# One core: shared weights in the local-attention value products, halves swapped for half of the heads, and one loop in place of two

## The reference, cut to what matters

```python
qkv = x @ Wqkv                      # 16 heads of 64
q, k = rotary(l2norm(q) * qs), rotary(l2norm(k) * ksc)
# windows of w = 32 tokens, so nw = 4 windows in 128 tokens
bk2, bv2 = look(bk), look(bv)       # each window sees itself and the window before it: 64 keys
mask = (it < jb) | (it > jb + w) | (jb == -1)
sim = where(mask, -max, einsum('bhwie,bhwje->bhwij', bq, bk2) * 8)
out = einsum('bhwij,bhwje->bhwie', softmax(sim), bv2)
x = out.reshape(b, n, 1024) @ Wo + x
```

## Time and profile before

| what | value |
|---|---|
| median of three runs | 1504.75 us |
| the profiled execution's own time | 1506.91 us |
| its span, first to last instruction | 1504.0 us |
| PE busy | 1419.3 us, 94% |
| DVE, ACT, POOL busy | 1310.1, 1269.5, 1179.5 us |
| `values`, records of L1246 on PE | 12288, 376.4 us busy (they overlap) |
| mean granted clock of TensorE | 0.985 |
| transfers `vs<-v` | 96 of 384 KB, 3.3 us to landing |

### The profile page before, as it was taken

How to read it: one execution, slowest core, us unless ns; L and a number is a source line. 1 busy time by engine, 2 the same in 40 slices (tenths; PEclk the granted TensorE clock), 3 DMA queues, 4 the chain that set the end, 5 groups by cost and what they waited for, 6 DMA issues and landing times.

```text
span 1504.0 us, 84580 instructions
## 1 busy us (share of the span) xinstructions
PE 1419.3 (94%) x33248; PEld 1150.9 (77%) x33248; DVE 1310.1 (87%) x2400; ACT 1269.5 (84%) x2523; POOL 1179.5 (78%) x1163
## 2 busy tenths in 40 slices
PE   6679999999999999999999999999999999999996
PEld 4457777778788787787878877787787877888875
DVE  5677899999999999999999999998999989999973
ACT  5467898988889888898988988888898878889883
POOL 2587788888888888788888888888888877788760
PEclk9699999999999999999999999999999999999999
DMA  4211100111110021011012001002100101110011
GB/s 135 70 40 37 40 27 27 49 47 51 40 42 27 27 62 57 27 44 38 27 38 81 27 27 52 30 27 81 38 21 23 40 23 36 55 31 21 25 39 29
DMA packets 41784, 62.44 MB, mean 42 GB/s; under 512 B 3854, under 2 KB 30732, under 8 KB 41740
## 3 DMA queue, kind: packets, MB, share of 16 engines
q1 hardware_dynamic: 41740, 61.84, 14.0%
HBM read 18.84 MB, written 1.05 MB: 13 GB/s over the span
## 4 chain that ended last, share of the span: by engine, by line
PE 89%; issue 4%; DVE 2%; ACT 1%; POOL 0%; DVEq 0%; ACTq 0%; POOLq 0%
PE bank L1179 12%; PE bank L1166 12%; PE bank L1246 11%; PE bank L1258 11%; PE bank L1219 10%; PE bank L1167 9%; PE bank L1168 9%; PE bank L1293 5%; PE bank L1282 3%; PE bank L1284 2%; PE bank L1283 2%; PE bank L1266 2%; PE bank L1272 2%; DVE u L896 1%; DVE t L905 1%
## 5 line engine op out<-in xcount | busy, mean ns | idle before, releaser
L422 POOL TENSOR_TENSOR u<-u,t 128x512 f32<-128x512 f32 x384 | 490.7, 1284 | 51.4 <-DVE t L905 51.0
L436 POOL TENSOR_TENSOR u<-u,rn 128x512 f32<-128x512 f32 x384 | 388.5, 1043 | 43.0 <-ACT rn L623 43.0
L1166 PE MATMUL bank<-Wl,xsh 128*128 (+1 forms) x576 | 271.5, 471 | 26.9 <-issue 11.7
L905 DVE TENSOR_TENSOR t<-bank,TS 128x512 f32<-128x512 f32 x384 | 262.5, 684 | 23.6 <-POOL u L422 18.4
L889 DVE TENSOR_REDUCE ss<-sq 128x8 f32<-128x512 f32 x384 | 253.9, 666 | 24.8 <-ACT sq L612 17.9
L612 ACT ACTIVATE sq<-bank 128x512 f32<-128x512 f32 x384 | 234.4, 611 | 39.8 <-PE bank L1168 38.7
L896 DVE TENSOR_TENSOR u<-bank,TC 128x512 f32<-128x512 f32 x384 | 257.3, 681 | 7.3 <-ACT sq L612 7.2
L442 POOL TENSOR_TENSOR P<-P,rs 128x512 f32<-128x512 f32 x192 | 198.6, 1045 | 72.5 <-DVE rs L933 72.5
L637 ACT COPY qkT<-bank 128x512 f32<-128x512 f32 x384 | 223.3, 615 | 12.9 <-PE bank L1179 12.3
L1168 PE MATMUL bank<-Wh,xsh 128*128 (+1 forms) x576 | 229.0, 398 | 0.0
L1167 PE MATMUL bank<-Wh,xsl 128*128 (+1 forms) x576 | 228.9, 397 | 0.0
(11 more groups left out here) (93 smaller groups left out, 2751.5 us busy)
## 6 DMA issues: line engine op xcount, KB each, us to landing
vs<-v SPq DMA_DIRECT2D x96, 384.0 KB, 3.3
Wraw<-in_L_ffn_Wqkv_dram SPq DMA_DIRECT2D x72, 117.5 KB, 2.1
WoS<-in_L_ffn_Wo_dram SPq DMA_DIRECT2D x6, 512.0 KB, 4.1
W1h<-Wh SPq DMA_DIRECT2D x6, 341.0 KB, 2.6
W1l<-Wl SPq DMA_DIRECT2D x6, 341.0 KB, 2.9
Wraw<-in_L_ffn_W_dram SPq DMA_DIRECT2D x12, 116.0 KB, 2.2
out_dram<-X SPq DMA_DIRECT2D x4, 256.0 KB, 2.3
W2S<-in_L_ffn_W_dram SPq DMA_DIRECT2D x6, 128.0 KB
```

Source lines behind the costliest of these rows:

```text
L422: nc.gpsimd.tensor_tensor(u[:, r, c], u[:, r, c], t2[:, r, c % 2], ALU.add).then_inc(add_done[c], 1)
L436: nc.gpsimd.tensor_tensor(by_head(u[:, r, c]), by_head(u[:, r, c]), spread(rn[:, r, HC * c:HC * c + HC], HC, DH), ALU.mult).then_inc(qk_re ...
L905: nc.vector.tensor_tensor(halves(t2[:, r, c % 2]), halves(bank_of("chunk", c, r)[:])[:, :, ::-1, :], TS[:, layer(it - lag), c % 2].broadca ...
L1166: nc.tensor.matmul(out, x[0], Wl[:, w], start=True, stop=False)
```

## The change

Five things are changed.

1. `values`: for each pair of heads and half of the partitions, 16 products now take windows 0 and 1 together, with the same weights (keys 0 to 63) and 64 moving columns in place of 32; 32 products take windows 2 and 3 one by one. That is 48 products a call in place of 64. Heads 8 to 15 have their halves swapped: their windows 0 and 1 lie in partitions 64 to 127.
2. `scores` writes to columns of the other half for s = 1, and window 0 now has its 32 keys in the first half of its 64 columns; the mask is 256 columns wide in place of 128, with swapped halves in the second 128 (`masks` reads it in another pattern, and shape_constants is a sixth longer); `o_out` writes through a pattern that swaps back.
3. `shifted_values`: four transfers of 64 partitions x 2 KB in place of one of 96 x 4 KB.
4. The two loops are one, over turns 3 to 47; the last eight turns convert weight blocks too (those of layer 5 again, read by nobody), and SP loads eight more blocks for it.
5. POOL's memset of `vs[0:32]` at the start is gone.

```diff
             def peeled(it):
-                step(it, lambda lag: 0 <= it - lag < PAIRS, split_lag <= it < split_lag + PAIRS - LAYER_PAIRS)
-            first, rest = LAST + 1, split_lag + PAIRS - LAYER_PAIRS
+                step(it, lambda lag: 0 <= it - lag < PAIRS, 0 <= it - split_lag < PAIRS)
+            first = LAST + 1
...
-            with eng.Fori(0, rest - first) as k:
+            with eng.Fori(0, PAIRS - first) as k:
                 step(k + first, lambda lag: True, True)
-            with eng.Fori(0, PAIRS - rest) as k:
-                step(k + rest, lambda lag: True, False)
...
-                l, b = divmod(k, NB // 2)
+                l, b = min(k // (NB // 2), L - 1), k % (NB // 2)
...
-                sp.dma_start(vs[32:128, n % 2], v[0:96, n % 2]).then_inc(vs_full, 16)
+                of, r = (slice(0, 512), slice(512, 1024)), n % 2
+                for dst, src in ((vs[64:128, r, of[0]], v[32:96, r, of[0]]), (vs[0:64, r, of[1]], v[32:96, r, of[1]]),
+                                 (vs[64:128, r, of[1]], v[0:64, r, of[1]]), (vs[0:64, r, of[0]], v[64:128, r, of[1]])):
+                    sp.dma_start(dst, src).then_inc(vs_full, 16)
...
-            nc.gpsimd.memset(vs[0:32], 0.0).then_inc(consts_done, 1)
...
-                    nc.scalar.copy(bank_of("scores", e, r)[:].rearrange("p (t n) -> p t n", t=4),
-                                   maskf[:].unsqueeze(1).broadcast_to([128, 4, 128])).then_inc(seeded[e], 1)
+                    nc.scalar.copy(bank_of("scores", e, r)[:].rearrange("p (s t n) -> p s t n", s=2, t=2),
+                                   maskf.unsqueeze(2).broadcast_to([128, 2, 2, 128])).then_inc(seeded[e], 1)
...
-                    nc.scalar.copy(OT[:, :, r, 64 * h:64 * h + 64],
-                                   bank_of("values", h, r)[:].rearrange("p (t c) -> p t c", c=64)).then_inc(OT_ready[h], 1)
+                    to = OT[:, 0, r, 64 * h:64 * h + 64]
+                    to = bass.AP(tensor=to.tensor, offset=to.offset,
+                                 ap=[to.ap[0], [8 * S + 64 * (1 - 2 * h), 2], [2 * S, 4], [1, 64]])
+                    nc.scalar.copy(to, bank_of("values", h, r)[:].rearrange("p (s t c) -> p s t c", s=2, t=4)
+                                   ).then_inc(OT_ready[h], 1)
...
-                                        at = 256 * s + 128 * t2_ + 64 * h
+                                        at = 256 * s + 128 * t2_ + 64 * (h ^ s)
...
-                    for t in range(INNER // 128):
-                        for w2 in range(2):
-                            for e in range(2):
-                                for h in range(2):
-                                    p, head = slice(64 * h, 64 * h + 64), (2 * t + e) * DH
-                                    at = 128 * (t // 2) + 64 * w2 + 32 * (t % 2)
-                                    i = nc.tensor.matmul(
-                                        bank_of("values", h, r)[64 * e:64 * e + 64, 64 * t + 32 * w2:64 * t + 32 * w2 + 32],
-                                        (vs, v)[w2][p, r, head:head + DH], PT[p, r, e, at:at + 32], start=True, stop=True)
+                    for blk in range(2):
+                        for a in range(2):
+                            for part in range(3):
+                                for e in range(2):
+                                    for h in range(2):
+                                        p, s = slice(64 * h, 64 * h + 64), (h if part == 0 else 1 - h)
+                                        t = 4 * s + 2 * blk + a
+                                        head, at = (2 * t + e) * DH, 128 * (t // 2) + 32 * a
+                                        to = bank_of("values", h, r)[64 * e:64 * e + 64, 64 * t:64 * t + 64]
+                                        if part == 0:
+                                            keys = (v, vs)[h][p, r, head:head + DH]
+                                            prob = PT[p, r, e, 128 * (t // 2):128 * (t // 2) + 128].rearrange(
+                                                "p (w a q) -> p w a q", w=2, a=2)[:, :, a]
+                                            to = to.rearrange("p (w q) -> p w q", w=2)
+                                        else:
+                                            at += 64 * (part - 1)
+                                            keys = (vs[p, r, head:head + DH] if part == 1 else v[p, r, head:head + DH] if h
+                                                    else vs[p, r, head - 512:head - 512 + DH])
+                                            prob, to = PT[p, r, e, at:at + 32], to[:, 32 * (part - 1):32 * part]
+                                        i = nc.tensor.matmul(to, keys, prob, start=True, stop=True)
```

More of the change, by code:

```diff
@@ L552, in first_upper @@
                 upper_part(k, k)
-            act.wait_ge(consts_done, 2)
+            act.wait_ge(consts_done, 1)
             act.wait_ge(bqs_ready, 1)
@@ L1378, in band_mask @@
     band = np.where((c < i) | (c > i + WINDOW), NEG, 0.0).astype(np.float32)
-    first = np.where(c < WINDOW, np.float32(NEG), band)
+    first = np.where(c > i, np.float32(NEG), np.float32(0))
     rows = [[first if (w2, wh) == (0, 0) else band for wh in range(2)] for w2 in range(2) for e in range(2)]
-    return np.concatenate([np.concatenate(r, 1) for r in rows], 0)
+    return np.concatenate([np.concatenate(r + r[::-1], 1) for r in rows], 0)
 _INS = ['x', 'ctx_1024', 'L0_ffn_Wqkv', 'L0_ffn_Wo', 'L0_ffn_W1', 'L0_ffn_W2']
```

13 lines of the change are left out of this document (7 added, 6 removed).

## The result

The changed kernel takes 1492.61 us (median of 9 runs, 1488.48 to 1496.61) against 1504.16 for the kernel before (median of 9, 1499.65 to 1509.49). The ratio is 0.9919, with a 95% interval of 0.9904 to 0.9934: 11.6 us less, or 0.8%. The forecast was 1502.0 with a range of 1489 to 1507, so the time lies in the range, but on the side to which I had given 0.20. Added up straight, the bounds of its terms reach from 1492.8 to 1511.2, so even the lowest of them lies just above what was measured.

A forecast was written before the change was run, and what follows sets the result against it. Chains on DVE and ACT beside the two values calls were taken to bound the plain turn, not PE's 94%. Terms -1.0 + 0 + 0 - 2.0 + 0.2 = -2.8 us, from 1504.75 to 1502.0; range 1489 to 1507.

The forecast's parts named there:

- Both calls have slack in the plain turn: Both values calls run beside chains that end PE's waits for chunk(1, 0, 0) and turn_qk(0, 0, 0); turns 3-47 gain 0.
- Rival (a): PE's saving is kept in the loop: 11 us a place, 1491, or 1480 with both; chance 0.15.
- Part 1, the size of the saving: Fewer products in values save PE 0.25 us of a call's 1.87, bounds 0 and 0.47.
- Part 1, the turns that run once: Uncovered turns: 0.6 us from fewer program stalls, 0.4 from two uncovered values calls; -1.0 us, bounds -4 and +2.
- Part 2: Mask, scores and result copy: new patterns leave copy times unchanged; 0 us, bounds -3.7 and +3.7.
- Rival (b): Copies to OT and the mask copy get slower in the new patterns: 1515.5 us; chance 0.05.
- Part 3: Four transfers of 128 KB for one of 384 KB land before values(1, 0) reads them, 6 us cover: 0.
- Part 4: One loop: no second entry, -4.5 us; conversions in turns 41 to 47, +2.5; sum -2.0, bounds -4.5 and +0.5.
- Rival (c): Turn 40's stall stays in some form and only conversions are added: 1506.5 us; chance 0.06.
- Part 5: The start: larger constants queue up to 0.7 us, taken as +0.2; the removed memset 0.

The follow-up runs named there:

- Experiments 5 to 11: Seven runs with steps reordered on DVE, ACT or both, in the kernel before or the changed one: 1482.16 to 1521.95 us.
- 6: Changed kernel, with DVE's swapped(3) and straight(3) moved ahead of squares(3): 1490.45 us.
- 7: Changed kernel, with ACT's two copies to OT moved ahead of the cast upper_x: 1503.21 us.
- 9: Changed kernel, with DVE's four steps reading the banks of chunks 3 and 0 put ahead of the sum of squares and row sums: 1482.16 us.
- experiment 3: Changed kernel, with each 64-column product of values issued as two of 32 columns: 1501.24 us.
- experiment 2: Kernel before, with only the two loops merged and the conversions that come with that: 1502.73 us.
- experiment 1: Changed kernel, with the two loops of before put back: 1491.36 us.
- experiment 11: Changed kernel, with DVE's order of 9 and ACT's copies to OT ahead of exp(0) and upper_x: 1487.4 us.
- 12: Changed kernel, with eight semaphore increments on PE behind each chunk of turn 0 (64 instructions without work): 1496.69 us.
- experiment 4: Changed kernel, with POOL's memset of vs[0:32] at the start put back: 1490.0 us.
- 5: Kernel before, with DVE's swapped(3) and straight(3) moved ahead of squares(3): 1504.71 us.

## Why the prediction held, and which term was mis-sized

The mechanism held. "Both calls have slack in the plain turn" came true: 35 turns moved by 0.2 us in all, with a saving on PE twice as large as forecast. The gaps ahead of both steps grew by what the calls lost (467 and 464 ns for 466), and the time from ACT's L613 to PE's next chunk stayed 2.93 us. PE's 94% in the earlier trace rows was no bound. Rival (a), the saving kept, fell by this. That its figure for one place, 1491, lies near the measured time is chance: its 11 us were to come from the loop. Experiments 5 to 11 show that these two waits alone do not set the turn: shortening either (6, 7) gains nothing, and the whole row of DVE (9) 0.2 us. What sets 29.04 us is not shown.

**Part 1, the size of the saving.** I took 0.25 us a call from a sum of 27 ns of columns and 31 of rest. It is 0.47, the upper bound. The failed assumption was that the price per column of a stream over the whole array adds to that of a small record. The Trainium skill, TensorEngine Tiling (Array Packing), Performance Considerations, has a rule of some 60 cycles a product, which would give the upper bound. The trace agrees in that 32 and 64 columns cost the same (58 ns a round); the 60 cycles themselves no run here shows. In the loop the error cost nothing.

**Part 1, the turns that run once.** This is the step that failed. "Of such stalls [...] I count 0.6 us, and 0.4 us for two calls", -1.0 us, with bounds of -4 and +2; turns 0 to 5 alone gave -7.4. Three things were missed. First, seven calls of `values` lie between turns 0 and 5, and some of these calls carry half-speed stretches and stalls inside them, where I had counted two calls, at full speed. The call that began at 125.18 took 3.13 us before and the one in its place takes 1.42; the next took 2.86 and takes 1.45; the next 2.08 and 1.38 (first to last start, from the records). Second, the stalls: those of 0.7 us or more past 97 us come to 7.2 us before (2.15, 1.71, 0.92, 0.72, 1.66) and 3.6 after (0.83, 1.55, 1.19). I had scaled them with the share of instructions removed, 7%; they halved. Third, the clock, in turn 2, which gave 4.9 of the 7.4 us. Its mean over the five turns is 0.93 in both kernels, but that hides where it fell. In turn 2 it is 0.90 before and 1.00 after:

```profile
52.80:201.80 149.00, 124.93 (x2772) 97.78 (x2773) 118.12 (x204) 106.27 (x211) 113.88 (x112) 0.93 0.13 38
```

```profile
50.00:191.60 141.60, 119.56 (x2548) 93.46 (x2549) 117.72 (x204) 105.62 (x211) 113.87 (x112) 0.93 0.17 48
```

```profile
106.20:140.50 34.30, 30.75 (x684) 24.71 (x685) 25.16 (x45) 26.16 (x52) 24.41 (x24) 0.90 0.11 33
```

```profile
102.40:131.80 29.40, 26.59 (x620) 21.70 (x621) 24.56 (x44) 25.71 (x52) 24.48 (x24) 1.00 0.18 47
```

The half-speed stretches of turn 2 before, 122.0 to 125.4 and 128.8 to 132.2 us, begin 1.0 and 0.9 us after a stop of PE ends (121.03 and 127.87). Turn 2 after has neither of these stops but the one that ends at 107.98, and no such stretch. What the stops cost by themselves, and what the clock cost, the runs do not separate.

How the 7.4 us divide depends on the order in which the parts are taken. With one loop the fewer records give 4.5 (experiment 3) and the merge the other 2.7 or so (experiment 2, 146.3 us for these turns). With two loops the changed `values` and all else but the merge give 149.0 - 140.8 = 8.2 (experiment 1) and the merge nothing. The stops ahead of turn 5 lie at the same records in the kernel before and in experiment 2, and four of the five are longer before (2.15 and 1.88 us ahead of record 820, 1.66 and 1.37 ahead of 2166). Why, no run shows.

Over turns 0 to 5 PE's busy time fell by 5.4 us and its idle time by 2.0; in a plain turn what busy time loses idle time gains.

**Part 2.** Right: in the loop the copies to `OT` take 593 ns and the mask copy 630 (589 and 630 in the earlier trace rows). Rival (b) fell.

**Part 3.** Right: four transfers of 128 KB, and no wait of PE for `vs` in the loop.

**Part 4.** Right in the trace (-2.3 for a forecast -2.0), but not a property of the merge alone: with the new `values` the second loop's entry would have cost 1.7 us and not 4.8 (experiment 1). The term was sized from an entry with two stops and a half-speed stretch, and with the new `values` it has one stop. Rival (c) fell: no turn past 5 is longer than 29.2 us.

**Part 5.** Forecast +0.2, measured -2.8, and this stays open. Kernels with the same start begin turn 0 anywhere from 48.3 (experiment 11) to 51.8 us (12); the memset is not it (experiment 4). One profile of each does not tell a cause from the scatter.

## What to carry to other kernels

Cut work on an engine that is 94% busy, and look at what ends its next wait: where that is a chain beside the work, the loop keeps its time, and the idle time grows by what was cut. So an engine's busy share does not tell what a cut is worth. Count the turns outside the loop apart: there less covers the engine, and another number of instructions also moves its waits for its own program, which can shorten them (here) or lengthen them (12). When the releaser of a wait is moved, move the whole row behind it in the order of its readers; moving one operation only handed the wait to the next step (5, 6, 7), and the whole row gained 0.2 us a turn (9).

## What of the hardware was not expected

A round of four products in the quarters of the array takes 58 ns with 32 and with 64 columns. Two kernels with equal numbers of matmuls and different work stop for their program at the same instructions, for 1.88 and 1.88, 1.70 and 1.72 us. 64 empty instructions ahead move two of the stops by 32 matmuls with their weight loads, and cost 4 us by the medians. Each of the stops followed here ends 2.2 to 3.0 us after a 16 KB transfer of instructions begins.
